# Step sizes as logarithms in the decay arguments, pair inputs as plain copies on ScalarE, output products ahead of the turn

## The chip, the cores and the metric

The kernel runs on one core of a Trainium2 chip. The metric is the device time of one launch in microseconds (us). The engines are named as in the profile: PE (matrix products and transposes; PEld is its weight load), DVE (vector), ACT (scalar functions and copies), POOL (GpSimd) and SP (issues the DMAs). They run side by side and wait for each other on semaphores.

## The reference, cut to what matters

Two batches of 1024 tokens with 256 features go through four blocks: local and global attention, a ternary feed-forward block, a state-space mixer with 64 heads, and a sum of eight factors. The change touches the mixer alone:

```python
dt = jax.nn.softplus(dt_raw + dt_bias)              # step size per token and head
a = jnp.exp(-jnp.exp(A_log) * dt)
phi = jnp.cumsum(dt, axis=1)[..., None] * rope_freqs
Bh = _rope(Bh, phi); Ch = _rope(Ch, phi)
u = xh * dt[..., None]
# per token:  h = a * h + u (outer) b ;  y = h . c
y = SSD_SCALE * ys + D_param[None, None, :, None] * xh
```

## The kernel before

Everything is written by hand: each engine has one program, and semaphores order them. A loop over the two batches holds the four blocks one after the other. In the mixer the 64 heads are worked in 32 pairs (`PAIRS`), one pair per **slot**; tokens are cut into chunks of 64 (`Q`). Ahead of the slots stands a **preparation**: `CUM` is the running sum of the step sizes, `LH` its product with the head's rate (the logarithm of the decay), `WH` the logarithm of the decay to a chunk's end. `LH` is split into three bf16 parts `LP`, stored to DRAM and loaded again in other layouts: `MV` (rows for the phases and the decays) and `NL` (the same decays as weights, for the source side of `exp(LH[t] - LH[s])`).

What each engine does in slot n, in program order:

- **DVE**: `products(n)` (L1152 to L1155, rotated B and C), `mixing(n-1)` (decay matrix times gram matrix, L1184, and the scan over chunk sums, L1189), `reduce_turns(n+2)` (L1139); in every second slot, from here on the odd one, also `pair_outputs` (L1198 to L1203) and `inputs` (L1169, L1173, L1177).
- **ACT**: `spread_decays` (L809), `whole_turns(n+2)` (L798), `turn_copy` 0 (L817), `sines(n+2)` (L804), `out_copy(n-1)` (L833), `decays(n)` (L825, an exponential), `turn_copy` 1 (L817). Sine and exponential each bring an ACT_TABLE_LOAD.
- **PE**: `turn` 0 (four transposes, L1531), `outputs(n-1)` (L1579, L1585), `decay_args(n)` (L1518, L1520), `gram` 0 (L1546), `turn` 1, `gram` 1, `phases(n+3)` (L1505), `chunk_sums(n)` (L1562), `turn_outputs(n-1)` (L1602).
- **POOL**: adds up the products: L635 for B (PE's `turn` waits for it), L636 for C (the `gram` and DVE's next `products` wait for it).
- **SP**: `swap(n+2)` (L527), four DMAs that exchange rows of the sines.

`inputs` writes what a pair of slots feeds to PE: `UI` is x times `DT8` (step size times 1/8), `US` is x times `DTW` (`DT8` times the decay to the chunk's end), and it multiplies x by `D_param` in place. The scratch `parts_d` is the DRAM copy of `LP`. `outputs(n-1)` waits for the scan of pair n-1 (`s_ss`); `products(n)` waits for `outputs(n-2)` (`s_yt`) and for POOL's L636 of slot n-1 (`s_bc`); `decay_args(n)` for `reduce_turns(n+2)` (`s_zw`); `phases(n+3)` for `decays(n)` (`s_de`), since they share two PSUM banks; `chunk_sums(n)` for `turn_copy` 1.

Of the kernel before, what the change touches and what calls it, by code (L numbers as in the profile page):

```python
# [21 lines left out]
F32 = mybir.dt.float32  # L22
# [8 lines left out]
ARENA = 39168  # L31
# [90 lines left out]
def build(nc, x, wq, wk, wv, wo, w_fc, w_proj, w_in, w_out, dt_bias, a_log, d_param, b_bias, c_bias, freqs, norm_w,  # L122
# [8 lines left out]
    with ctx:  # L131
# [131 lines left out]
        DT8 = arena.take(NT, HEADS)  # L263
        DTW = arena.take(NT, HEADS)
# [14 lines left out]
        LRES = arena.take(T)  # L279
# [4 lines left out]
        RST = arena.take(T)  # L284
# [28 lines left out]
        parts_d = nc.dram_tensor("parts_scratch", (P, 4, T), BF16, kind="Internal").ap()  # L313
        turns_d = nc.dram_tensor("turns_scratch", (PAIRS, 3, 8, P), BF16, kind="Internal").ap()
# [75 lines left out]
        s_lp = sem("parts_ready")  # L390
        s_lc = sem("chunk_decays_masked")
# [57 lines left out]
        def _(sp):  # L449
# [37 lines left out]
            with sp.Fori(0, NB) as b:  # L487
# [25 lines left out]
                for lo, hi, done in ((0, 1, s_mv0), (1, PAIRS // 4, s_mv)):  # L513
                    for q in range(3):
                        sp.dma_start(MV[32 * q:32 * q + 32, lo:hi], cum[:, lo:hi]).then_inc(done, 16)
                    sp.dma_start(MV[96:128, lo:hi], low[:, lo:hi]).then_inc(done, 16)
                    if lo == 0:
                        for a in range(3):
                            sp.dma_start(NL[64 + 16 * a:80 + 16 * a], parts_d[HEADS:, a].rearrange("h (k s) -> k h s", s=Q)
                                         ).then_inc(s_nl, 16)  # L520
# [27 lines left out]
        def _(pool):  # L548
# [45 lines left out]
            with pool.Fori(0, NB) as b:  # L594
# [29 lines left out]
                for half in range(2):  # L624
# [4 lines left out]
                    pool.drain().then_inc(s_hs, 1)  # L629
                def slots(it):  # L630
# [13 lines left out]
        def _(act):  # L644
# [29 lines left out]
            with act.Fori(0, NB) as b:  # L674
# [105 lines left out]
                nc.scalar.activation(DTE, DTE, ACT.Ln, bias=1.0).then_inc(s_lg, 1)  # L780
                act.wait_ge(s_lh, b + 1)
# [52 lines left out]

                def slots(it, first, last):
                    for k in range(4):
# [10 lines left out]
                        turn_copy(n, k, 1)  # L847

                for k in range(2):
                    whole_turns(k, k)  # L850
                    sines(k, k)
                slots(0, True, False)
# [26 lines left out]
        def _(dve):  # L879
# [103 lines left out]
            with dve.Fori(0, NB) as b:  # L983
# [85 lines left out]
                for u in range(2 * HK):  # L1069
# [22 lines left out]
                nc.vector.scalar_tensor_tensor(DT[:, :, 0], DTA, 0.0, DTE, ALU.max, ALU.add)  # L1092
                nc.vector.scalar_tensor_tensor(DT[:, :, 1], DTA, 0.0, DTE, ALU.max, ALU.add).then_inc(s_dt, 1)
# [6 lines left out]
                nc.vector.tensor_tensor_scan(CUM, RST, PS[:, 4:6, :].rearrange("p k t -> p (k t)"), 0.0, ALU.mult, ALU.add)  # L1100
# [3 lines left out]
                lh = LH[64:128].rearrange("h (k s) -> h k s", s=Q)  # L1104
                nc.vector.tensor_tensor(WH[64:128].rearrange("h (k s) -> h k s", s=Q),
                                        lh[:, :, Q - 1:Q].to_broadcast([HEADS, T // Q, Q]), lh, ALU.subtract).then_inc(s_lh, 1)
# [25 lines left out]
                nc.vector.tensor_tensor(DTW, DT8, WT, ALU.mult).then_inc(s_prep, 1)  # L1132
# [24 lines left out]
                def inputs(n, k):  # L1157

                    dve.wait_ge(s_zc, at(b, n, 3))
                    dve.wait_ge(s_yt, at(b, n, 3))  # L1160
                    m = k // 2 % 2
                    x = XS[:, :, bass.ds(n * 16, 32)]
                    each = x.rearrange("p t (r h d) -> p t r h d", r=2, h=2)
                    all4 = x.rearrange("p t (e d) -> p t e d", d=HD)
                    for c in range(2):
                        for h in range(2):
                            q, t = slice(64 * c, 64 * c + 64), slice(64 * h, 64 * h + 64)
                            f = DT8[q, :, bass.ds(n * 2, 4)].rearrange("p t (r h) -> p t r h", h=2)[:, :, :, h]
                            nc.vector.tensor_tensor(UI[t, 2 * m:2 * m + 2, c, h].rearrange("p r d t -> p t r d"),  # L1169
                                                    each[q, :, :, h], f.unsqueeze(3).to_broadcast([64, NT, 2, HD]), ALU.mult)  # L1170
                    for c in range(2):
                        q = slice(64 * c, 64 * c + 64)
                        nc.vector.tensor_tensor(US[q, m, :, :, :, :, c].rearrange("p t r h d -> p t (r h) d"), all4[q],  # L1173
                                                DTW[q, :, bass.ds(n * 2, 4)].unsqueeze(3).to_broadcast([64, NT, 4, HD]), ALU.mult)
                    dve.drain()
                    d = dpar[:, bass.ds(n * 2, 4)].unsqueeze(1).unsqueeze(3).to_broadcast([P, NT, 4, HD])
                    nc.vector.tensor_tensor(all4, all4, d, ALU.mult).then_inc(s_u, 2)  # L1177

# [14 lines left out]
                def pair_outputs(n):  # L1193
# [3 lines left out]
                    y = PS[:, 7, :].rearrange("p (y t e d) -> p y t e d", y=2, t=NT, d=HD)  # L1197
                    nc.vector.tensor_tensor(YT, y[:, 0], e, ALU.mult)  # L1198
# [3 lines left out]
                    own = XS[:, :, bass.ds(n * 16, 32)].rearrange("p t (e d) -> p t e d", d=HD)  # L1202
                    nc.vector.tensor_tensor(own, own, YT, ALU.add).then_inc(s_yd, 2)  # L1203

                def slots(it, first, last):
                    for k in range(4):
# [8 lines left out]
                        if k % 2 == 1 and not (last and k == 3):  # L1215
                            inputs(n + 1, k + 1)
# [512 lines left out]
```

## Time and profile before

| | |
|---|---|
| median of 3 runs | 1911.16 us (1909.46 to 1920.73) |
| the profiled execution | 1920.04 us, span 1918.2 us |
| mean granted PE clock | 0.803 of full |
| busy in the span | PE 1342.2, PEld 799.2, DVE 1227.5, ACT 909.1, POOL 407.5 us |
| first and last slot of the first batch begin at | 522.2 and 888.8 us |
| first and last slot of the second batch begin at | 1449.8 and 1815.5 us |

The span is the time from the first instruction to the last. An engine's busy time is a sum over stages with different limits, so it does not tell what limits the slots; for that the timeline of one pair of slots is read. A row's bracket gives the idle time of the engine before it and what ended it.

### The profile page before, as it was taken

The numbers are of one execution on the slowest core, as the hardware profiler recorded it, in microseconds if no ns is written. First come the engines' busy times: TensorE is split into PE (matmuls) and PEld (weight loads), VectorE is DVE, ScalarE is ACT, GpSimd is POOL, SyncE is SP. The second block draws the span as 40 slices with busy tenths as digits, with TensorE's granted clock in tenths as the row PEclk, the third lists the DMA queues.
The fourth block names the chain that finished last, engine by engine and source line by source line (L and its number), as shares of the span: only waits on it lengthen the run. The fifth ranks groups of instructions, "written<-read, shape, count | busy, mean of one in ns | idle before, by whom it ended". The sixth has DMA issues, their size and how long they took to land.

```text
span 1918.2 us, 40292 instructions
## 1 busy us (share of the span) xinstructions
PE 1342.2 (70%) x14984; PEld 799.2 (42%) x14984; DVE 1227.5 (64%) x2325; ACT 909.1 (47%) x1424; POOL 407.5 (21%) x322
## 2 busy tenths in 40 slices
PE   0368898595377777777637788859565777777782
PEld 0253332243155555555425333214233555555562
DVE  7456781413788888886455577342457888888836
ACT  0273456232466666664317245533145666666540
POOL 6210000020043333343012000002002333333400
PEclk9677999797577777778867689979776887777795
DMA  4300000100411111111010000010013121111100
GB/s 158 95 1 2 2 2 1 44 1 11 91 45 46 44 44 44 44 44 24 1 45 1 2 2 2 2 44 1 11 36 87 45 47 44 44 44 44 34 1 22
DMA packets 36685, 62.42 MB, mean 33 GB/s; under 512 B 15040, under 2 KB 24000, under 8 KB 35792
## 3 DMA queue, kind: packets, MB, share of 16 engines
q1 hardware_dynamic: 36272, 58.70, 12.4%
q8 instruction: 74, 1.21, 0.3%
q10 hardware_dynamic: 288, 2.10, 0.3%
q14 instruction: 51, 0.42, 0.1%
HBM read 20.79 MB, written 6.23 MB: 14 GB/s over the span
## 4 chain that ended last, share of the span: by engine, by line
issue 75%; POOL 15%; DVE 3%; POOLq 3%; PE 3%; DVEq 1%; DMA 0%; ACT 0%; SPq 0%
POOL region L636 8%; POOL region L635 6%; POOLq L628 2%; POOL region L620 1%; PE PS L1649 1%; PE PS L1664 1%; PE PS L1670 1%; DMA region<-in_L_ffn_W_proj_dram 0%; DVE fsum L976 0%; POOLq L601 0%; DVE bst L885 0%; DVE X L937 0%; DVE region L963 0%; DVE region L971 0%; DVE region L966 0%
## 5 line engine op out<-in xcount | busy, mean ns | idle before, releaser
L635 POOL TENSOR_TENSOR region<-region 128x1024 f32<-128x1024 f32 x64 | 150.8, 2356 | 655.2 <-DVE region L1155 655.2
L1018 DVE TENSOR_REDUCE region<-PS 128x1 f32<-128x512 f32 (+3 forms) x304 | 180.6, 654 | 81.5 <-PE PS L1352 44.3
L1531 PE MATMUL PS<-ident,region 128*128 128x128 f32 x512 | 102.4, 333 | 175.8 <-POOL region L635 175.8
L716 ACT ACTIVATE region<-PS 128x512 f32<-128x512 f32 x288 | 164.0, 597 | 129.1 <-PE PS L1399 88.0
L1546 PEld LDWEIGHTS PS<-region 64*64 64x64 f32 x4096 | 144.6, 141 | 47.5 <-issue 47.5
L1546 PE MATMUL PS<-region 64*64 64x64 f32 x4096 | 162.2, 230 | 0.0
L627 POOL TENSOR_TENSOR region<-region 128x512 f32<-128x512 f32 x28 | 35.4, 1265 | 553.2 <-ACT region L758 552.3
L1152 DVE SCALAR_TENSOR_TENSOR region<-region,rows 128x1024 f32<-128x1024 f32 x64 | 82.2, 1285 | 109.9 <-PE PS L1585 90.5
L1288 PE MATMUL PS<-ident,S 128*128 128x128 f32 x128 | 35.0, 429 | 167.8 <-DVE S L915 164.8
L636 POOL TENSOR_TENSOR region<-region 128x1024 f32<-128x1024 f32 x64 | 151.7, 2370 | 0.0
L817 ACT COPY region<-PS 128x512 f32<-128x512 f32 x128 | 74.9, 585 | 159.3 <-PE PS L1531 158.8
L1531 PEld LDWEIGHTS PS<-ident,region 128*128 128x128 f32 x512 | 65.0, 163 | 190.5 <-POOL region L635 94.6
L798 ACT ACTIVATE region<-PS,roundc 128x1024 f32<-128x1024 f32 x64 | 71.3, 1114 | 135.9 <-DVE region L1155 121.7
L1349 PE MATMUL PS<-region 96*128 96x512 bf16 (+3 forms) x384 | 116.4, 354 | 23.8 <-DVE region L1018 15.8
L1399 PE MATMUL PS<-region 99*128 99x512 bf16 x288 | 113.0, 415 | 18.9 <-ACT region L716 17.8
L649 ACT COPY XT<-PS 128x256 f32<-128x256 f32 x64 | 23.8, 372 | 168.0 <-PE PS L1288 166.2
L1288 PEld LDWEIGHTS PS<-ident,S 128*128 128x128 f32 x128 | 19.3, 203 | 183.3 <-DVE S L915 175.8
L1337 PE MATMUL PS<-region 128*32 128x512 f32 x576 | 86.7, 666 | 0.2
L1139 DVE SCALAR_TENSOR_TENSOR region<-region,PS 128x1024 f32<-128x1024 f32 x64 | 76.8, 1200 | 12.7 <-ACT region L798 12.7
L1184 DVE TENSOR_TENSOR S<-PS,region 128x1024 f32<-128x1024 f32 x64 | 78.1, 1221 | 9.7 <-PE PS L1546 9.0
L1155 DVE SCALAR_TENSOR_TENSOR region<-region,rows 128x1024 f32<-128x1024 f32 x64 | 81.9, 1280 | 0.0
L1154 DVE SCALAR_TENSOR_TENSOR region<-region,rows 128x1024 f32<-128x1024 f32 x64 | 81.9, 1280 | 0.0
(246 smaller groups left out, 2960.1 us busy)
## 6 DMA issues: line engine op xcount, KB each, us to landing
region<-region SPq DMA_DIRECT2D x256, 128.0 KB, 2.3
region<-parts_scratch SPq DMA_DIRECT2D x8, 448.0 KB, 9.2
region<-in_L_ffn_factors_dram SPq DMA_DIRECT2D x2, 1024.0 KB, 7.3
X<-in_L_attn_x_dram SPq DMA_DIRECT2D x2, 1024.0 KB, 5.9
region<-w1T_scratch SPq DMA_DIRECT2D x2, 1024.0 KB, 4.8
region<-w2T_scratch SPq DMA_DIRECT2D x2, 1024.0 KB, 6.9
out_dram<-X SPq DMA_DIRECT2D x2, 1024.0 KB, 4.9
parts_scratch<-region SPq DMA_DIRECT2D x2, 768.0 KB, 3.2
```

Source lines behind the costliest of these rows:

```text
L635: nc.gpsimd.tensor_tensor(PB1[:, r], PB1[:, r], PB2, ALU.add).then_inc(s_bb, 1)
L636: nc.gpsimd.tensor_tensor(PC1[:, r], PC1[:, r], PC2, ALU.add).then_inc(s_bc, 1)
L716: nc.scalar.activation(PB[:, u % (2 * G0), :], PS[:, 2 + u % 2, :], ACT.Exp).then_inc(s_p, 1)
L1018: nc.vector.reduce_max(MB[:, h:h + nh, k0 // 4], src, AX).then_inc(s_smu, 1)
L1152: nc.vector.scalar_tensor_tensor(PB1[:, k % 2], XV[:, 0], g(0), T1[:, k % 2], ALU.add, ALU.mult)
L1154: nc.vector.scalar_tensor_tensor(PC1[:, k % 2], XV[:, 2], g(2), T1[:, k % 2], ALU.add, ALU.mult)
L1155: nc.vector.scalar_tensor_tensor(PC2, XV[:, 3], g(3), T2[:, k % 2], ALU.add, ALU.mult).then_inc(s_pm, 1)
L1337: mm(PS[32 * g:32 * g + 32, 4, :], V[:, j, g, :], PB[:, v % (2 * G0), :], start=j == 0, stop=j == i, tile_position=(0, 32 * g), skip_group ...
L1349: last = mm(o, QT[0:SPLIT, h + q, i * P:(i + 1) * P], KT[0:SPLIT, (h + q) // HPG, k0 * P:(k0 + nk) * P], start=True, stop=not diag, skip_g ...
L1399: last = mm(o, KT[:, g, j * P:(j + 1) * P], QT[:, g * HPG:(g + 1) * HPG, i * P:(i + 1) * P], start=True, stop=j != i)
L1531: last = tr(PS[:, 4, (i % 4) * P:(i % 4 + 1) * P], PB1[:, r, i * P:(i + 1) * P], ident[:])
L1546: last = mm(PS[q, 2 + half, (i % 4) * P + 64 * c:(i % 4) * P + 64 * c + 64], PB1[q, r, t], PC1[q, r, t], start=True, stop=True, tile_posit ...
```

## The change

Three things are changed. First, the step size leaves the inputs: `exp(LH[t] - LH[s]) * dt[s] / 8` becomes `exp(LH[t] - (LH[s] - log(dt[s] / 8)))`. The preparation gains a logarithm on ACT (`LN`), a subtraction on DVE (`LS`), a split of `LS` into three bf16 parts on POOL (`LQ`), and a DRAM round trip of its own for the source side (`sources_d`, then `NL`), and SP issues that after all loads of `MV`. `XW`, x times the decay to the chunk's end, is made once for all heads on DVE. Second, `inputs` then only copies, and moves from DVE to the end of the odd slots on ACT; the product with `D_param` goes into DVE's `pair_outputs`. Third, PE does `outputs(n-1)` ahead of `turn` 0 in a slot.

```diff
 (SP, preparation: the NL loads no longer stand between the first and the other loads of MV)
+                sp.wait_ge(s_lq, b + 1)
+                sp.dma_start(sources_d, LQ[64:128]).then_inc(s_lqs, 16)
+                sp.wait_ge(s_lqs, (b + 1) * 16)
+                for a in range(3):
+                    sp.dma_start(NL[64 + 16 * a:80 + 16 * a], sources_d[:, a].rearrange("h (k s) -> k h s", s=Q)
+                                 ).then_inc(s_nl, 16)
 (POOL, preparation)
+                pool.wait_ge(s_lh, b + 1)
+                nc.gpsimd.tensor_tensor(LQ[64:128, 0], LS[64:128], onesc[64:128].to_broadcast([HEADS, T]), ALU.mult)
+                pool.drain()
+                nc.gpsimd.tensor_tensor(LS[64:128], LS[64:128], LQ[64:128, 0], ALU.subtract)
+                pool.drain()
+                nc.gpsimd.tensor_copy(LQ[64:128, 1], LS[64:128])
+                pool.drain()
+                nc.gpsimd.tensor_tensor(LQ[64:128, 2], LS[64:128], LQ[64:128, 1], ALU.subtract).then_inc(s_lq, 1)
 (ACT, preparation)
+                act.wait_ge(s_cum, b + 1)
+                nc.scalar.activation(LN[64:128], PS[64:128, 4:6, :].rearrange("p k t -> p (k t)"), ACT.Ln,
+                                     scale=float(NS) ** -0.5).then_inc(s_ln, 1)
 (ACT, at the end of a slot with k = 1 or 3)
+                    for c in range(2):
+                        for h in range(2):
+                            nc.scalar.copy(UI[t, 2 * m:2 * m + 2, c, h].rearrange("p r d t -> p t r d"), x[q, :, :, h])
+                    for c in range(2):
+                        last = nc.scalar.copy(US[q, m, :, :, :, :, c].rearrange("p t r h d -> p t (r h) d"), w[q])
 (DVE, preparation)
-                nc.vector.tensor_scalar(DT8, DT[:, :, 0], float(NS) ** -0.5, None, ALU.mult)
+                dve.wait_ge(s_ln, b + 1)
+                nc.vector.tensor_tensor(LS[64:128], LH[64:128], LN[64:128], ALU.subtract)
...
-                nc.vector.tensor_tensor(DTW, DT8, WT, ALU.mult).then_inc(s_prep, 1)
+                nc.vector.tensor_tensor(XW.rearrange("p t (h d) -> p (t h) d", d=HD), XS.rearrange("p t (h d) -> p (t h) d", d=HD),
+                                        WT.rearrange("p t h -> p (t h)").unsqueeze(2).to_broadcast([P, NT * HEADS, HD]),
+                                        ALU.mult).then_inc(s_prep, 1)
 (DVE, slots: inputs is gone; in pair_outputs)
                     nc.vector.tensor_tensor(YT, y[:, 0], e, ALU.mult)
+                    nc.vector.tensor_tensor(own, own, d, ALU.mult)
                     dve.drain()
 (PE, slots)
-                        turn(n, k, 0)
                         if not (first and k == 0):
                             outputs(n - 1, k + 3)
+                        turn(n, k, 0)
                         decay_args(it, k, not (last_ and k >= 2))
```

In the order of PE's instructions this is the beginning of a slot inside the loop; before (`PS<-ident,region` is `turn`, 32x128 are `outputs`, 128x512 are `decay_args`, 64x64 is `gram`):

```order
L1531 MATMUL PS<-ident,region 128x128 x4
L1579 MATMUL PS<-region 32x128 x8
L1585 MATMUL PS<-S,region 32x128 x8
...
L1518 MATMUL PS<-region 128x512
L1520 MATMUL PS<-region 128x512
L1518 MATMUL PS<-region 128x512
L1520 MATMUL PS<-region 128x512
L1546 MATMUL PS<-region 64x64 x16
```

and after:

```order
L1602 MATMUL PS<-region 32x128 x8
L1608 MATMUL PS<-S,region 32x128 x8
L1551 ISA
L1554 MATMUL PS<-ident,region 128x128 x4
...
L1541 MATMUL PS<-region 128x512
L1543 MATMUL PS<-region 128x512
L1541 MATMUL PS<-region 128x512
L1543 MATMUL PS<-region 128x512
L1569 MATMUL PS<-region 64x64 x16
```

The sixteen `outputs` products moved ahead of the four transposes; the rest of the slot stands as it stood.

On ACT the end of an odd slot and the beginning of the next, after the change (`x4` and `x2` are the new copies to `UI` and `US`, L838 is `turn_copy`, L830 `spread_decays`, L819 `whole_turns`):

```order
L846 ACTIVATE region<-PS 128x1024
L835 REGISTER_ALU
L838 COPY region<-PS 128x512
L865 COPY region<-region 64x8x2x8 x4
L869 COPY region<-region 64x256 x2
L830 COPY region<-region 128x16x15
L816 REGISTER_ALU
L819 ACTIVATE region<-PS,roundc 128x1024
```

Before, `spread_decays` followed `turn_copy` 1 at once. On SP, in the preparation, before:

```order
L507 DMA parts_scratch<-region 128x3072
L509 REGISTER_ALU
L515 DMA region<-parts_scratch 32x1024 x3
L516 DMA region<-parts_scratch 32x1024
L519 DMA region<-parts_scratch 16x64x64 x3
L515 DMA region<-parts_scratch 32x7x1024 x3
L516 DMA region<-parts_scratch 32x7x1024
L525 ISA
L527 DMA region<-region 32x1024 x4
```

and after:

```order
L513 DMA parts_scratch<-region 128x3072
L515 REGISTER_ALU
L521 DMA region<-parts_scratch 32x1024 x3
L522 DMA region<-parts_scratch 32x1024
L521 DMA region<-parts_scratch 32x7x1024 x3
L522 DMA region<-parts_scratch 32x7x1024
L525 DMA sources_scratch<-region 64x3072
L528 DMA region<-sources_scratch 16x64x64 x3
L534 ISA
L536 DMA region<-region 32x1024 x4
```

The three loads of `NL` (16x64x64) moved behind the big loads of `MV` and behind a store of their own, and stand directly ahead of the first `swap`.

## Rows read from the trace of the kernel before

**Rows 1.** What DVE waited for before the first product of a slot (us, times).

```profile
L1152 DVE SCALAR_TENSOR_TENSOR region<-region,rows x64: 1279/1285/1287, 522.2 to 1815.5; 128x1024 f32<-128x1024 f32 x64
...
  PE PS L1585: 90.5, 30
```

**Rows 2.** Timeline, DVE: first and last slot of batch one, first of two.

```profile
522.18 1.28 DVE L1152 SCALAR_TENSOR_TENSOR region<-region,rows 128x1024 f32<-128x1024 f32 x1 [3.73 <-DMA region<-region]
...
888.82 1.28 DVE L1152 SCALAR_TENSOR_TENSOR region<-region,rows 128x1024 f32<-128x1024 f32 x1 [3.95 <-PE PS L1585]
...
1449.78 1.28 DVE L1152 SCALAR_TENSOR_TENSOR region<-region,rows 128x1024 f32<-128x1024 f32 x1 [3.06 <-DMA region<-region]
```

**Rows 3.** Timeline of an even slot (start, duration in us, engine, line).

```profile
715.17 1.28 DVE L1155 SCALAR_TENSOR_TENSOR region<-region,rows 128x1024 f32<-128x1024 f32 x1
...
718.84 2.37 POOL L636 TENSOR_TENSOR region<-region 128x1024 f32<-128x1024 f32 x1
...
719.02 1.11 PE L1531 MATMUL PS<-ident,region 128*128 128x128 f32 x4 [4.75 <-POOL region L635]
...
720.06 1.11 PE L1579 MATMUL PS<-region 128*32 128x128 f32 x16
...
721.96 0.61 PE L1518 MATMUL PS<-region 112*128 112x512 bf16 x1
...
722.30 1.28 DVE L1152 SCALAR_TENSOR_TENSOR region<-region,rows 128x1024 f32<-128x1024 f32 x1 [3.00 <-PE PS L1585]
...
727.58 1.10 PE L1562 MATMUL PS<-region 128*64 128x16 f32 x32
```

**Rows 4.** Timeline of the odd slot that follows.

```profile
728.73 0.69 DVE L1189 TENSOR_TENSOR_SCAN region<-region,PS 128x256 f32<-128x256 f32 x1 [0.36 <-PE PS L1562]
...
729.67 0.66 PE L1531 MATMUL PS<-ident,region 128*128 128x128 f32 x4 [0.42 <-POOL region L635]
730.25 0.45 PEld L1579 LDWEIGHTS PS<-region 128*32 128x32 f32 x16 [0.17 <-issue]
...
731.37 0.39 PE L1518 MATMUL PS<-region 112*128 112x512 bf16 x1
...
731.52 0.72 DVE L1203 TENSOR_TENSOR region<-region 128x256 f32 x1 [0.17 <-issue]
...
732.17 1.59 DVE L1169 TENSOR_TENSOR region<-region 64x128 f32 x4
...
734.06 1.20 PE L1546 MATMUL PS<-region 64*64 64x64 f32 x32
...
735.24 1.28 DVE L1152 SCALAR_TENSOR_TENSOR region<-region,rows 128x1024 f32<-128x1024 f32 x1
...
736.42 0.60 PE L1505 MATMUL PS<-region 96*128 x2 [1.17 <-ACT region L825]
736.49 0.41 ACT L809 COPY region<-region 128x240 f32 x1
...
736.95 1.11 PE L1562 MATMUL PS<-region 128*64 128x16 f32 x32
```

**Rows 5.** Two windows: length, busy per engine, then granted clock, DMA, GB/s.

```profile
714.50:724.70 10.20, 5.68 (x57) 3.54 (x59) 7.20 (x8) 5.60 (x6) 4.67 (x2) 0.50 0.05 11
724.80:738.30 13.50, 11.91 (x260) 9.32 (x258) 12.64 (x18) 9.60 (x13) 4.71 (x2) 1.00 0.30 68
```

**Rows 6.** Timeline, batch two: POOL's addition and DVE's input products beside it.

```profile
1466.85 2.38 POOL L636 TENSOR_TENSOR region<-region 128x1024 f32<-128x1024 f32 x1
...
1467.21 3.47 DVE L1169 TENSOR_TENSOR region<-region 64x128 f32<-64x128 f32 x4
```

**Rows 7.** Timeline, preparation of batch one: DVE, the subtraction to WH.

```profile
492.14 1.22 DVE L1105 TENSOR_TENSOR region<-region 64x1024 f32<-64x1024 f32 x1
```

**Rows 8.** DMA issues by line (count, KB each, us to landing).

```profile
parts_scratch<-region SPq DMA_DIRECT2D x2, 768.0 KB, 3.2
...
region<-parts_scratch SPq DMA_DIRECT2D x6, 128.0 KB, 4.8
```

More of the change, by code:

```diff
@@ L30 @@
 BLOCKS = 4
-ARENA = 39168
+ARENA = 41984
 C = 256
@@ L262, in build @@
         XV = arena.take(4, T)
-        DT8 = arena.take(NT, HEADS)
-        DTW = arena.take(NT, HEADS)
+        XW = arena.take(NT, DI)
         ELT = arena.take(NT, HEADS)
@@ L278, in build @@
         LH = arena.take(T)
-        LRES = arena.take(T)
+        LRES = BSQ.rearrange("p t n -> p (t n)")
         LP = arena.take(3, T, dt=BF16)
@@ L283, in build @@
         LCH = arena.take(PAIRS, T // Q)
-        RST = arena.take(T)
+        LQ = arena.take(3, T, dt=BF16)
+        RST = LQ.rearrange("p q t -> p (q t)").bitcast(F32)[:, 0:T]
+        LN, LS = WH, CUM
         prep_used = arena.used
@@ L390, in build @@
         s_lp = sem("parts_ready")
+        s_cum = sem("sums_of_steps_ready")
+        s_ln = sem("log_steps_ready")
+        s_lq = sem("source_parts_ready")
+        s_lqs = sem("source_parts_stored")
         s_lc = sem("chunk_decays_masked")
@@ L833, in out_copy, with inputs @@
                     nc.scalar.copy(YC[:, k % 2], PS[:, 6, :]).then_inc(s_yc, 1)
+                def inputs(n, k):
+                    act.wait_ge(s_zc, at(b, n, 3))
+                    act.wait_ge(s_yt, at(b, n, 3))
+                    m = k // 2 % 2
+                    x = XS[:, :, bass.ds(n * 16, 32)].rearrange("p t (r h d) -> p t r h d", r=2, h=2)
+                    for c in range(2):
+                        for h in range(2):
+                            q, t = slice(64 * c, 64 * c + 64), slice(64 * h, 64 * h + 64)
+                            nc.scalar.copy(UI[t, 2 * m:2 * m + 2, c, h].rearrange("p r d t -> p t r d"), x[q, :, :, h])
+                    w = XW[:, :, bass.ds(n * 16, 32)].rearrange("p t (e d) -> p t e d", d=HD)
+                    for c in range(2):
+                        q = slice(64 * c, 64 * c + 64)
+                        last = nc.scalar.copy(US[q, m, :, :, :, :, c].rearrange("p t r h d -> p t (r h) d"), w[q])
+                    last.then_inc(s_u, 2)
                 def slots(it, first, last):
@@ L847, in slots @@
                         turn_copy(n, k, 1)
+                        if k % 2 == 1 and not (last and k == 3):
+                            inputs(n + 1, k + 1)
                 for k in range(2):
@@ L851, in _ @@
                     sines(k, k)
+                act.wait_ge(s_prep, b + 1)
+                inputs(0, 0)
                 slots(0, True, False)
@@ L1155, in products @@
                     nc.vector.scalar_tensor_tensor(PC2, XV[:, 3], g(3), T2[:, k % 2], ALU.add, ALU.mult).then_inc(s_pm, 1)
[L1157 to L1177, printed above, removed]
                 def mixing(n, k):
@@ L1214, in slots @@
                             pair_outputs(n - 3)
-                        if k % 2 == 1 and not (last and k == 3):
-                            inputs(n + 1, k + 1)
                 reduce_turns(0, 0)
                 reduce_turns(1, 1)
-                inputs(0, 0)
                 slots(0, True, False)
```

21 lines of the change are left out of this document (10 added, 11 removed).

## The prediction

> **What bounds the kernel now.** I look first at DVE's first product of a slot. It began 366.64 us after the first in the last slot of batch one (31 slots, 11.83 us each), and in batch two from 1449.78 to 1815.5, 11.80 each [rows 1, 2]. So 62 slot steps of 11.81 us hold 732 of the 1920 us; two slots are 23.6 us. Next I ask what DVE waited for there: 90.5 us in 30 slots for PE's outputs [rows 1]. The timeline shows the chain of a pair. DVE's products end at 716.45 (715.17 + 1.28); POOL adds for 2 x 2.4 us, to 721.21; PE turns B from 719.02, does the outputs from 720.06 to 721.96, and DVE goes on at 722.30 after 3.00 us idle [rows 3]. Then DVE works almost without a gap until the next products at 735.24, the last 3.07 us of it inputs (from 732.17) [rows 4]. Neither PE nor ACT is full: ACT is busy 5.60 + 9.60 = 15.2 us of the pair [rows 5]. The pair is one chain: products, POOL, turn, outputs, products, inputs.
>
> **Part one: inputs leave DVE.** DVE loses 3.07 us in an odd slot and gains the product with D_param in pair_outputs, 256 elements, some 0.4 us. That product reads two operands in SBUF. Such an operation stands still beside POOL: four input products took 3.47 us beside L636 against 1.59 alone, and L1203 took 0.72 [rows 4, 6]. Pair_outputs starts some 3.3 us after the products' end, L636 ends 4.76 after it (721.21 - 716.45), so the product and the two operations behind it end near 4.76 + 0.3 + 0.5 + 0.5 = 6.0; with products of 4.87 an odd slot needs 10.9 us on DVE. An even slot needs L636 and then products: 4.76 + 0.1 + 4.87 = 9.7. DVE and POOL alone would allow 20.6 per pair, 10.3 per slot.
>
> **Part two: six copies on ACT.** The nearest row is a copy of 240 elements, 0.41 us [rows 4]; six of those are 2.46. DVE's own figure, 1.59 + 0.85, is the same. Four of the copies have only 128 elements, so I take 2.2, with 2.0 to 2.5 as bounds; in slots 15.2 + 2.2 = 17.4 us per pair, under the 20.6. They stand beside work of others: from turn_copy 1 to the next turn_copy 0, ACT has 2.2 + 0.41 + 1.1 = 3.7 us, while PE and DVE have chunk sums, scan, outputs and turn, 0.3 + 1.11 + 0.8 + 1.1 + 0.7 = 4.0. Cover for 0.3; beyond 2.5 us every tenth would show. The Trainium skill (ScalarE: Activation LUTs, section "What ACT_TABLE_LOAD costs") gives an ACTIVATE 186 ns plus 0.833 ns per element, less 93 when back to back; by that estimate the six take 1.4 us, and the cover would be 1.1. No number here uses it.
>
> **Part three: outputs first.** DVE's 3.00 us shrink only to the next lock, L636 at 4.76, so 2.0. But a new ring closes: scan, outputs, turn, ACT's copies, sine and exponential, phases, chunk sums, scan. Before, the turn waited for POOL alone. At the high clock: outputs 731.37 - 730.25 = 1.12; turn to the end of the chunk sums 729.67 to 738.06 = 8.39, all of it ACT's sequence and what PE hangs on it; scan 0.69 plus 0.2 of semaphores [rows 4]. Sum **10.4 us** per slot, just over DVE's 10.3. At the low clock outputs take 721.96 - 720.06 = 1.90, and turn to end of chunk sums 719.02 to 728.68 = 9.66 [rows 3]: 1.90 + 9.66 + 0.89 = **12.45**. In between, with only outputs and turn low: 1.12 becomes 1.90 and the turn 1.11 instead of 0.66, so 10.4 + 0.78 + 0.45 = **11.63**.
>
> **The clock decides.** It is the high level (2.4 GHz) from 724.8 to 738.3 and the low one (1.2) from 714.5 to 724.7 [rows 5]. It fell at 738.3 after PE had idled 1.17 us for the exponential and then done only phases, chunk sums and turn_outputs, and rose 5.7 us after work began at 719.02. In the new ring at the high clock PE's gram ends 735.26 - 729.67 = 5.59 after the old turn; without the outputs between, 4.5. The phases start 6.75 after the turn (736.42 - 729.67): a hole of 2.2 us, then the same light work. So I expect a fall in most slots that began at the high clock; the next slot then has outputs and turn at the low one, its gram ends about when the exponential does, the hole closes and the clock comes back. Half high at 10.4 and half at 11.63 gives 11.0; I take **11.05**. Loop: 62 x (11.81 - 11.05) = **-47 us**.
>
> **Part four: the preparation.** It ends, before, with DVE waiting 3.73 us for the first swap, behind the loads of MV in the queue [rows 2]. Per batch:
> DVE gains the subtraction LS, 1.2 us [rows 7]; the logarithm (1.0, like an exponential of the size) runs beside LH; DT8 goes, -0.3. Together +1.2 ahead of LP.
> POOL gains three additions and a copy over 1024 elements, 4 x 2.4 = 9.5 us, beside five DVE operations on LP, two or three of them with both operands in SBUF. By rows 6 each of those waits out a POOL operation: two to three waits of 2.4, 4.7 to 7.1; 0 if POOL comes late. I take 6. The Trainium skill (SBUF — State Buffer, section "Who interferes with whom") makes the pair of ports an exclusive lock for a whole instruction and adds that casts in a two-port mode take it too; by that the two casts to LP wait as well, and the estimate is the upper bound, 7.1. No row here shows a cast beside POOL.
> SP now waits for the store of LQ behind all MV loads: a round trip like that of LP, 3.2 us [rows 8], half the bytes. The NL loads (4.8 us [rows 8]) and the swap follow as before, only later.
> XW is a product of 4096 elements, four times 1.2 less overheads, 4.4 us instead of 0.7: hidden behind the queue, which is then some ten us late; without that cover it would cost 3.7.
> Sum 1.2 + 6 + 3.2 = 10.4 per batch (4.4 to 12): **+21 us**.
>
> **Forecast.** Against the profiled 1920.04 us (its span is 1918.2) the sum is -26; it stands 9 us over the median, inside the runs' spread, and I carry the -26 over: 1911 - 26 = **1885 us**, own range 1870 to 1900. Less than 1%, 19 us, cannot be told from no change here.
>
> **Rivals.**
> (a) The clock stays high: the fall above came with DVE idle for another 4.75 us behind it, and the new ring has no such pause. For it: 10.4 per slot; 62 x 1.41 = 87, less 21: 1911 - 66 = 1845. Against: the clock fell at 738.3 before that pause had its turn. 27%.
> (b) Every slot at 11.63, the hole not closing: 62 x 0.18 = 11 off, 21 on: 1921, no change. 13%.
> (c) Slower: outputs now run in front of turn, decay_args and gram, all at the low clock, and PE itself becomes the ring. If slots alternate between 11.63 and 12.45, mean 12.04: +14 and +21, 1946. It decides from a mean slot of 11.5, where the loop no longer pays for the preparation; +1% is reached at 11.8. For: at the low clock the gram ended after the exponential in rows 3's slot. Against: without a hole PE is busy, and in rows 5 that brought the clock back. 11%.
> (d) The strided copies cost twice the rows, 4.4 us: 1.9 over the cover, in 31 pair steps of both batches 59 us on top of the forecast: 1944. Against: DVE's 1.59 already holds the strided writes. 6%.
> The forecast keeps 43%.
>
> **How the numbers follow.** Faster by over 1% (under 1892) holds (a) and three quarters of the forecast's share: 0.58. Same (to 1930): the rest of it and (b): 0.25. Slower: (c), (d): 0.17. The range leaves out the tail beyond (a) and that beyond (c): 1840 to 1945.
>
> **What the changed profile would show.** Steps of 11.0 us between first products, alternating by about 1.2; PE's first outputs row waiting for DVE's scan, not for POOL; the granted clock in the loop near 0.8 and low at outputs; six ACT copies of 2.0 to 2.5 us together, and no wait of DVE for whole_turns; DVE's LRES and LP operations stretched beside POOL, and the first products some 10 us later after LP's store. The forecast is wrong if the slots are at 10.4 or over 11.5, or if the preparation moves by less than 3 us or more than 13.

## The result, and the profile after

The changed kernel takes **1922.49 us** (median of 12 runs, 1917.98 to 1930.04), the kernel before 1911.88 beside it (12 runs, 1906.02 to 1920.73). The ratio is 1.0054, 95% interval [1.0035, 1.0073]. It is a little slower and not, as forecast, faster. The profiled execution has a span of 1925.8 us at a mean granted clock of 0.807 (before 1918.2 and 0.803).

The timeline of DVE in the changed kernel, four single answers: the first product of the first and the last slot of batch one, then of batch two. They answer to [rows 2].

```profile
532.32 1.28 DVE L1198 SCALAR_TENSOR_TENSOR region<-region,rows 128x1024 f32<-128x1024 f32 x1 [8.98 <-DMA region<-region]
...
894.29 1.28 DVE L1198 SCALAR_TENSOR_TENSOR region<-region,rows 128x1024 f32<-128x1024 f32 x1 [2.36 <-PE PS L1608]
...
1462.40 1.28 DVE L1198 SCALAR_TENSOR_TENSOR region<-region,rows 128x1024 f32<-128x1024 f32 x1 [7.90 <-DMA region<-region]
...
1822.66 1.28 DVE L1198 SCALAR_TENSOR_TENSOR region<-region,rows 128x1024 f32<-128x1024 f32 x1 [2.36 <-PE PS L1608]
```

31 slots in 361.97 and 360.26 us are steps of 11.68 and 11.62 us. Before they were 11.83 and 11.80: the loop gained 4.7 and 5.4 us per batch, 10 in all, where 47 were forecast. Most of that lies in its start: the first four steps of a batch took 45.9 us before and 41.4 and 41.5 now, while from the eighth slot on the mean step went from 11.94 and 11.91 to 11.89 and 11.88. The loop once it runs has gained next to nothing. The preparation, from the start of the cumulative scan at 489.33 (L1140) to the first product, took 532.32 - 489.33 = 43.0 us, and 41.9 in batch two; before it was 33.2 and 32.5. That is 19 us more. The two together, 9 us more, are the result.

The loop first. What DVE waited for before L1198, whole span (us, times); it answers to [rows 1], where 90.5 us in 30 slots stood:

```profile
L1198 DVE SCALAR_TENSOR_TENSOR region<-region,rows x64: 1277/1284/1286, 532.3 to 1822.7; 128x1024 f32<-128x1024 f32 x64
...
  PE PS L1608: 12.8, 15
  POOL region L654: 9.3, 5
```

The wait that outputs first was made for is down to a seventh. The same view for `phases` on PE (it adds the idle time of PE's weight load) shows another:

```profile
L1528 PE MATMUL PS<-region x128: 379/387/634, 516.0 to 1806.3; 96*128 x96, 96*128 96x512 bf16 x32
...
  ACT region L846: 122.3, 64
```

Before, this row read 20.1 us in 21. PE alone, counted in the timeline, now waits for ACT's exponential (L846) ahead of 56 of the 58 `phases` inside the slots, 108 us, 1.9 us each; before it was 17 us ahead of 17 of them. The timeline of an odd slot with its predecessor's end shows what hangs on it. It answers to [rows 3, 4]: L1554 is `turn`, L1602 and L1608 `outputs`, L1585 `chunk_sums`, L1213 DVE's scan.

```profile
721.86 1.00 PE L1528 MATMUL PS<-region 96*128 x2 [2.25 <-ACT region L846]
...
722.06 1.75 ACT L865 COPY region<-region 64x128 f32 x4
...
722.78 1.88 PE L1585 MATMUL PS<-region 128*64 128x16 f32 x32
723.82 0.86 ACT L869 COPY region<-region 64x256 f32 x2
...
724.71 0.69 DVE L1213 TENSOR_TENSOR_SCAN region<-region,PS 128x256 f32<-128x256 f32 x1 [1.55 <-PE PS L1585]
...
725.60 1.11 PE L1602 MATMUL PS<-region 128*32 128x128 f32 x16
...
727.49 1.11 PE L1554 MATMUL PS<-ident,region 128*128 128x128 f32 x4
...
731.26 1.20 PE L1569 MATMUL PS<-region 64*64 64x64 f32 x32
...
733.38 1.02 ACT L846 ACTIVATE region<-PS 128x1024 f32<-128x1024 f32 x1
...
734.57 0.60 PE L1528 MATMUL PS<-region 96*128 x2 [2.11 <-ACT region L846]
...
735.10 1.51 PE L1585 MATMUL PS<-region 128*64 128x16 f32 x32
...
736.65 0.69 DVE L1213 TENSOR_TENSOR_SCAN region<-region,PS 128x256 f32<-128x256 f32 x1 [0.93 <-PE PS L1585]
...
737.53 1.11 PE L1602 MATMUL PS<-region 128*32 128x128 f32 x16
...
739.25 0.65 PE L1554 MATMUL PS<-ident,region 128*128 128x128 f32 x4
```

From turn to turn it is 739.25 - 727.49 = 11.76 us. PE ends its gram at 732.46 and stands idle until 734.57. In the kernel before, in the slot of [rows 3], the second gram ended at 727.11, 8.09 us after the turn, and `phases` (L1505) came without a hole:

```profile
725.91 1.20 PE L1546 MATMUL PS<-region 64*64 64x64 f32 x32
...
727.04 0.60 PE L1505 MATMUL PS<-region 96*128 x2
```

Windows of the changed kernel's stretch (length, busy of PE, PEld, DVE, ACT, POOL, granted clock, DMA share, GB/s; they answer to [rows 5]):

```profile
721.90:728.60 6.70, 6.70 (x87) 5.23 (x88) 3.89 (x4) 4.13 (x9) 4.33 (x2) 0.50 0.09 20
729.00:735.40 6.40, 4.27 (x82) 3.05 (x83) 4.62 (x5) 6.20 (x9) 2.61 (x2) 1.00 0.36 82
736.00:738.90 2.90, 2.90 (x56) 2.74 (x58) 2.25 (x4) 0.43 (x1) 1.45 (x1) 0.50 0.00 0
```

In this slot the clock is at 2.4 GHz for decay arguments, grams, hole and `phases`, and at 1.2 GHz for most of the chunk sums and for the outputs. In the slot before it `phases`, chunk sums and outputs all ran at 1.2. That is the work that the ring runs through.

The preparation, timeline of batch one in the changed kernel. L1159 and L1161 are DVE's last operations on the way to `LP`, L640 begins the split on POOL, L1176 is `XW`, L525 the source's store, L528 the loads of `NL`, L536 the swaps.

```profile
495.31 2.40 POOL L640 TENSOR_TENSOR region<-region,onesc 64x1024 bf16<-64x1024 f32 x1 [74.30 <-DVE region L1149]
...
501.66 1.31 DVE L1159 CAST region<-region 128x1024 bf16<-128x1024 f32 x1
...
503.05 2.99 DVE L1161 TENSOR_TENSOR region<-region 128x1024 bf16<-128x1024 f32 x1
...
513.01 0.81 SPq L525 DMA_DIRECT2D sources_scratch<-region  x1
...
514.29 4.42 DVE L1176 TENSOR_TENSOR region<-region 128x4096 f32<-128x4096 f32 x1
...
523.89 1.63 SPq L528 DMA_DIRECT2D region<-sources_scratch  x3
...
525.65 19.33 SPq L536 DMA_DIRECT2D region<-region  x12
```

`LP` is complete at 506.04, 16.7 us after the scan's start (before 10.2). The source's store is issued behind the loads of `MV`, its `NL` loads 10.9 us later, and the first swap behind those.

### The profile page after: what moved, and what is told of

Same layout as the page of the kernel before. It is cut to its first block, busy times and chain, and to the rows that moved or that the text cites. A ratio compares the mean times of both kernels' runs of the same rounds, so it can differ in the third digit from the quotient of the medians.

```text
span 1925.8 us, 40168 instructions
## 1 busy us (share of the span) xinstructions
PE 1360.6 (71%) x14904; PEld 840.1 (44%) x14984; DVE 1162.5 (60%) x2133; ACT 987.4 (51%) x1618; POOL 425.9 (22%) x330
## 3 DMA queue, kind: packets, MB, share of 16 engines
q1 hardware_dynamic: 36432, 59.48, 12.5%
## 4 chain that ended last, share of the span: by engine, by line
issue 65%; PE 11%; POOL 8%; ACT 6%; DVE 4%; POOLq 4%; DVEq 1%; DMA 0%; ACTq 0%; SPq 0%
POOL region L654 4%; POOL region L653 3%; PE PS L1585 2%; POOLq L637 2%; ACT L825 2%; PE PS L1602 2%; PE PS L1554 2%; ACT L846 2%; ACT region L846 2%; PE PS L1608 1%; PE PS L1625 1%; POOL region L629 1%; PE PS L1528 1%; PE PS L1672 1%; ACT region L854 1%
## 5 line engine op out<-in xcount | busy, mean ns | idle before, releaser
L838 ACT COPY region<-PS 128x512 f32<-128x512 f32 x128 | 74.6, 583 | 189.8 <-PE PS L1554 189.8
L1569 PEld LDWEIGHTS PS<-region 64*64 64x64 f32 x4096 | 137.3, 135 | 44.5 <-issue 44.5
L1569 PE MATMUL PS<-region 64*64 64x64 f32 x4096 | 154.8, 224 | 1.2 <-issue 1.1
L1528 PE MATMUL PS<-region 96*128 (+1 forms) x128 | 45.4, 442 | 121.6 <-ACT region L846 108.2
L1554 PE MATMUL PS<-ident,region 128*128 128x128 f32 x512 | 104.1, 337 | 29.8 <-POOL region L653 29.8
L1198 DVE SCALAR_TENSOR_TENSOR region<-region,rows 128x1024 f32<-128x1024 f32 x64 | 82.1, 1283 | 46.3 <-DMA region<-region 16.9
L1585 PEld LDWEIGHTS PS<-region 128*64 128x64 f32 x2048 | 88.5, 178 | 34.0 <-ACT region L838 31.5
L1585 PE MATMUL PS<-region 128*64 128x16 f32 (+1 forms) x2048 | 94.4, 237 | 5.2 <-ACT region L838 5.2
L1554 PEld LDWEIGHTS PS<-ident,region 128*128 128x128 f32 x512 | 66.8, 167 | 57.1 <-issue 52.7
```

Source lines behind the costliest of these rows:

```text
L1198: nc.vector.scalar_tensor_tensor(PB1[:, k % 2], XV[:, 0], g(0), T1[:, k % 2], ALU.add, ALU.mult)
L1554: last = tr(PS[:, 4, (i % 4) * P:(i % 4 + 1) * P], PB1[:, r, i * P:(i + 1) * P], ident[:])
L1569: last = mm(PS[q, 2 + half, (i % 4) * P + 64 * c:(i % 4) * P + 64 * c + 64], PB1[q, r, t], PC1[q, r, t], start=True, stop=True, tile_posit ...
L1585: last = mm(to[:, 8 * h:8 * h + 8, 2 * i:2 * i + w], BT[:, r, i, 64 * h:64 * h + 64], US[:, m, i, r, h, :, 0:w], start=True, stop=True, ti ...
```

## Experiments

Ten kernels ran, each timed in three rounds beside the kernel before. "Slot" is the mean step between first products of batch one and two, "preparation" the time from the scan's start to the first product, both read as above; the clock is the mean of the profiled execution. A ratio is to the kernel before in the same rounds (1913.6 to 1914.6 us for e1 to e10).

| kernel | median us | ratio [95%] | slot | preparation | clock |
|---|---|---|---|---|---|
| before | 1911.9 | 1 | 11.83, 11.80 | 33.2, 32.5 | 0.803 |
| changed | 1922.5 | 1.0054 [1.0035, 1.0073] | 11.68, 11.62 | 43.0, 41.9 | 0.807 |
| e1 | 1867.8 | 0.9775 [0.9741, 0.9810] | 10.79, 10.83 | 42.9, 41.8 | 0.832 |
| e2 | 1914.7 | 1.0013 [0.9989, 1.0037] | 11.86, 11.88 | 31.7, 33.1 | 0.817 |
| e3 | 1867.2 | 0.9768 [0.9737, 0.9799] | 10.62, 10.62 | 41.1, 41.4 | 0.882 |
| e4 | 1912.5 | 0.9993 [0.9967, 1.0018] | 11.67, 11.66 | 37.1, 37.1 | 0.807 |
| e5 | 1862.8 | 0.9725 [0.9683, 0.9766] | 10.77, 10.73 | 37.1, 37.1 | 0.824 |
| e6 | 1860.6 | 0.9712 [0.9668, 0.9756] | 10.77, 10.80 | 37.1, 37.4 | 0.829 |
| e7 | 1859.0 | 0.9720 [0.9680, 0.9760] | 10.63, 10.72 | 37.1, 37.1 | 0.831 |
| e8 | 1853.8 | 0.9681 [0.9641, 0.9722] | 10.67, 10.71 | 37.1, 37.1 | 0.846 |
| e9 | 1860.8 | 0.9732 [0.9681, 0.9783] | 10.72, 10.68 | 39.1, 39.5 | 0.852 |
| e10 | 1860.7 | 0.9724 [0.9672, 0.9775] | 10.64, 10.64 | 39.5, 39.6 | 0.875 |

Slot and preparation come from one profiled execution each. What lies outside of them took 1106 to 1125 us in these twelve executions, so a difference of a few us between medians of four or five runs need not come from the edit. The profiled execution lies under its kernel's median by 12 us in e3 and by 8 in e9, and over it by 9 in e8 and by 5 in e5.

**e1: the changed kernel with PE's old order.**

```diff
+                        turn(n, k, 0)
                         if not (first and k == 0):
                             outputs(n - 1, k + 3)
-                        turn(n, k, 0)
```

> The changed kernel with PE's turn ahead of the outputs in a slot, as before the change; all else as changed. Theory R (the ring through outputs): a slot of the changed kernel is as long as the ring scan, outputs, turn, ACT's sequence, phases, chunk sums, scan, 11.65 us on average. With turn first the outputs leave the ring and also fill part of PE's hole ahead of the phases. Expected: 10.6 to 11.2 us per slot, so 28 to 65 us less than the changed kernel's 1922: 1857 to 1894 us. Rival L (DVE beside POOL's lock, or ACT with its six copies, sets the slot): the order on PE does not matter, 1915 to 1925 us.

One moved call takes 55 us off the changed kernel. The theory of the ring held: preparation as before the edit, slot 0.8 us shorter. PE's wait before `phases` fell from 122.3 to 32.2 us in the view above. In the odd slots DVE and POOL show as the limit that part one of the prediction described; timeline of one:

```profile
716.85 2.38 POOL L654 TENSOR_TENSOR region<-region 128x1024 f32<-128x1024 f32 x1
...
717.55 1.97 DVE L1225 TENSOR_TENSOR region<-region,dpar  x1
...
720.54 1.28 DVE L1198 SCALAR_TENSOR_TENSOR region<-region,rows 128x1024 f32<-128x1024 f32 x1
```

The product with `D_param` takes 1.97 us beside POOL and 0.41 without it (738.70 in the changed kernel). The step to the next products is 10.96 us, with DVE at work all the time; part one gave 10.9. In the even slots DVE still waited for PE's outputs, 25 us in 10 of the last 24 slots of batch one.

**e2: the kernel before with outputs first, and nothing else.**

```diff
-                        turn(n, k, 0)
                         if not (first and k == 0):
                             outputs(n - 1, k + 3)
+                        turn(n, k, 0)
```

> The kernel before with nothing changed but PE's order: outputs ahead of turn. Theory R: the ring of 11.6 us per slot (clock low at phases, chunk sums, outputs) now bounds the even slots that took 10.7, and the odd slots stay at DVE's 12.9: a pair of 24.0 to 24.5 us against 23.6, 10 to 28 us slower, 1922 to 1940 us. Rival G (the reorder is what its place suggests, a shorter way from POOL to DVE's products): DVE's 3.0 us of idle time shrink to 2.0, 1880 to 1895 us.

No gain, and the time, 1914.7, lies below the theory's range and far above the rival's. DVE's wait fell only to POOL's addition, and the hole ahead of `phases` (here L1505) opened. Timeline, the end of an odd slot and the even one behind it:

```profile
704.93 1.28 DVE L1152 SCALAR_TENSOR_TENSOR region<-region,rows 128x1024 f32<-128x1024 f32 x1 [0.60 <-PE PS L1546]
...
706.62 1.03 PE L1505 MATMUL PS<-region 96*128 x2 [2.25 <-ACT region L825]
...
714.71 1.28 DVE L1152 SCALAR_TENSOR_TENSOR region<-region,rows 128x1024 f32<-128x1024 f32 x1 [2.06 <-POOL region L636]
```

From the even slot's first product to the next slot's it is 9.78 us; the odd slot behind it takes 13.9, and the pair is at 23.7 as before. The theory had the ring lengthen the even slot; the odd one lengthened and the even one shortened. With e1 this makes a square. Everything but the order, mainly inputs on ACT, is worth 1.0 us per slot with turn first (before to e1) and 0.2 with outputs first (e2 to changed); the order by itself brings nothing, and with the copies it takes most of their gain away.

**e3: PE's hole filled.** Sixteen products go to columns of `PS` that nothing reads in the slots; they compute nothing that is used.

```diff
                         gram(n, k, 1)
+                        for _ in range(16):
+                            mm(PS[:, 5, 272:512], identb[:], masks[:, 0:240], start=True, stop=True)
```

> The changed kernel with sixteen extra bf16 products of 240 columns on PE behind the second gram of every slot, written to columns of PSUM that nothing reads: they fill the hole in which PE waits for the exponential. Theory C (the clock): the ring is 10.4 us at the high clock, and what makes it 11.65 is that the clock falls in or behind the hole, so that phases, chunk sums and outputs run at the low one. Expected: granted clock in the slots over 0.95, phases 0.6, chunk sums 1.1, outputs 1.1 us, slots of 10.3 to 10.7 us, 1840 to 1870 us. Rival N (the ring's length is set by ACT and the semaphores, not by the clock): the extra products only delay the phases, 1922 to 1960 us.

Work that is useless takes 55 us off, as theory C gave and against rival N. Windows and timeline of e3:

```profile
532.00:890.00 358.00, 315.87 (x5617) 246.97 (x5618) 273.58 (x287) 276.52 (x385) 149.12 (x64) 0.99 0.20 45
```

```profile
719.37 1.81 PE L1640 MATMUL PS<-masks,identb 128*128 128x240 bf16 x16
721.81 0.60 PE L1528 MATMUL PS<-region 96*128 x2 [0.63 <-ACT region L846]
722.35 1.10 PE L1585 MATMUL PS<-region 128*64 128x16 f32 x32
...
724.24 0.70 PE L1602 MATMUL PS<-region 128*32 128x128 f32 x16 [0.23 <-DVE region L1213]
...
725.36 0.66 PE L1554 MATMUL PS<-ident,region 128*128 128x128 f32 x4
```

In the loop of batch one the granted clock is 0.99, where the changed kernel had 0.79. From `phases` to the turn it is 725.36 - 721.81 = 3.55 us; the changed kernel had 727.49 - 721.86 = 5.63 and 739.25 - 734.57 = 4.68. That is where the slot's time went. What is left here of DVE's idle time is, in the last 24 slots of batch one, 21.5 us in 11 slots for `whole_turns`, which stands behind the six copies on ACT, and 20.6 in 19 for the chunk sums.

**e4: the split on POOL waits for `LP`.**

```diff
-                pool.wait_ge(s_lh, b + 1)
+                pool.wait_ge(s_lp, b + 1)
```

> The changed kernel with POOL's split of LS waiting until DVE has finished LP, so that its four operations no longer run beside DVE's operations on SBUF operands. Theory P (POOL holds DVE up in the preparation): LP is stored 5 to 6 us earlier in each batch, the split is ready at about the time at which SP has issued the loads of MV, and the kernel takes 9 to 12 us less than the changed one: 1910 to 1914 us. Rival Q (the DMA queue alone sets when the first products start): under 3 us, 1919 to 1923 us.

Theory P held. `LP` was complete 11.65 us after the scan's start, not 16.7: 5.06 us were contention. The preparation took 5.9 and 4.9 us less, and the median 10.0. The loop stayed as it was. The contention did not vanish, it moved, to small operations with one array and one column as operands (L1161 ends `LP`, L1171 is such an operation):

```profile
503.71 1.23 DVE L1161 TENSOR_TENSOR region<-region 128x1024 bf16<-128x1024 f32 x1
...
505.05 1.91 DVE L1171 TENSOR_SCALAR region<-region,rstd 128x64 f32<-128x64 f32 x1
```

The 48 of them took from 504.85 to 519.51, 14.7 us, against 8.3 in the changed kernel (505.96 to 514.29).

**e5: e1 and e4 together.** Diffs as there.

> The changed kernel with PE's turn first and with POOL's split waiting for LP: the two edits of the first runs together. Both are in different stages, so they should add: the slots of 10.8 us of the run with the turn first (1868) and a preparation of 37.1 us instead of 42. Expected 1856 to 1862 us. Rival: the preparation's gain is lost when the first slots wait for something else, 1866 to 1870.

Slot of e1, preparation of e4: in the profile the two add up. The median, 1862.8, is just above the expected range.

**e6: e5, and the large loads of `MV` issued behind the first two swaps.**

```diff
+                load_rows(0, 1, s_mv0)
...
                 swap(0, 0)
                 swap(1, 1)
+                load_rows(1, PAIRS // 4, s_mv)
```

> The run before (turn first, split late) with the big loads of MV issued behind the first two swaps instead of ahead of the sources' round trip. Theory Q: what remains of the longer preparation is the queue, in which the first swap stands behind the MV loads, a store's round trip and NL. Expected: first products some 30 us after the start of the running sum instead of 37, 14 us less in all, 1842 to 1848 us. Rival: the preparation is then set by DVE's product XW, the sines and the NL loads, and gains less than 3 us per batch, 1853 or more.

A miss: the queue was cleared and the preparation stayed at 37.1. The timeline of e6 (lines three further on: L1179 is `XW`, L1188 `reduce_turns`, L828 the sine, L538 the swap, L530 the `NL` loads):

```profile
507.93 1.53 SPq L530 DMA_DIRECT2D region<-sources_scratch  x3
...
511.24 4.41 DVE L1179 TENSOR_TENSOR region<-region 128x4096 f32<-128x4096 f32 x1
...
515.57 1.20 DVE L1188 SCALAR_TENSOR_TENSOR region<-region,PS 128x1024 f32<-128x1024 f32 x1
...
516.81 1.06 ACT L828 ACTIVATE region<-region 128x1024 f32<-128x1024 f32 x1 [0.69 <-DVE region L1188]
...
517.89 5.90 SPq L538 DMA_DIRECT2D region<-region  x8
...
522.10 1.28 DVE L1201 SCALAR_TENSOR_TENSOR region<-region,rows 128x1024 f32<-128x1024 f32 x1 [1.83 <-DMA region<-region]
```

Nothing stood in the queue when the sine ended; the swap went out at once. The limit was engines' work, DVE's chain of small operations, `XW` and `reduce_turns`, then the sine. It had been so since e4: there too `XW` began 26.2 us after the scan's start (at 519.51), and the swap went out at 526.17, when the sine was done. The edit cleared a queue that no longer set the time.

**e7: e6, with the ACT copies behind `whole_turns`** in the even slots instead of at the end of the odd ones (`inputs(n, k)` ahead of `turn_copy(n, k, 0)`).

> The run before with ACT's six copies moved from the end of the odd slot to the next slot behind whole_turns, ahead of the turn's copy. Theory A: at 2.6 us the copies outlast their cover and hold back whole_turns, so DVE's reduce_turns and PE's decay arguments start late in every even slot (DVE waited 0.7 us for ACT there, 2.1 with the high clock). With whole_turns first that wait goes: slots of 10.5 instead of 10.8 us, 12 to 22 us less than the run before, 1822 to 1834. Rival: the copies then stand before the turn's copy, which opens ACT's sequence, and delay it by as much: no change within 5 us, or slower.

A miss; the rival held. The slots are shorter by 0.14 and 0.07 us, the median by 1.5; the intervals overlap, and no gain is shown. DVE's wait for `whole_turns` did go (7.7 us in the last 24 slots of e6's batch one, none here), but its wait for POOL's addition ahead of the products grew from 2.3 to 16.2.

**e8: e7 with eight filling products** at e3's place.

> The run before with eight extra bf16 products of 240 columns behind the second gram (half of those of the first such run, since the outputs already stand in the slot's first half). Theory C: the clock still falls in part of the slots with the turn first (0.83 over the kernel), and with the hole half filled it stays high: granted clock in the slots over 0.95 and 10.2 to 10.4 us per slot, 6 to 18 us less than the run before. Rival: with the turn first PE's hole is no longer in the ring and the clock does not matter, no change or some us slower.

A miss: the loop's clock rose from 0.87 (e7) to 0.92 and not over 0.95, and the slot did not get shorter. The rival fits. The median is the lowest of all, 3.2% under the kernel before; that it beats e5 to e7 is not shown, since the intervals overlap and loop and preparation together of both batches are as in e7 (736.8 against 736.0 us). Windows of e8 and, in the second line, of e10 below:

```profile
532.00:880.00 348.00, 296.44 (x5306) 221.56 (x5306) 282.13 (x284) 270.76 (x369) 150.10 (x64) 0.92 0.23 51
...
532.00:880.00 348.00, 302.10 (x5533) 239.63 (x5566) 271.20 (x283) 270.38 (x369) 150.47 (x64) 0.99 0.21 48
```

**e9: e8 with `XW` behind the first two `reduce_turns`.** The array `WT` that it reads lies elsewhere in memory, and a drain follows it.

```diff
-                nc.vector.tensor_tensor(XW ... )
...
                 reduce_turns(0, 0)
                 reduce_turns(1, 1)
+                nc.vector.tensor_tensor(XW ... )
```

> The kernel of e8 with DVE's product XW (4.4 us) moved behind the first two reduce_turns, ahead of the first products; the array that it reads is placed elsewhere, so that the first swap may land before XW has ended. Theory D, the preparation is set by DVE's own chain: in e6 XW ended at 515.65, reduce_turns followed at 515.57, the sine at 516.81, the swap was issued at 517.89 and had landed by 522.10. Without XW in that chain the swap is issued 4.4 us sooner, XW lies beside sine and swap, and the preparation takes 37.1 - 4.4 = 32.7 us per batch (31.5 to 34), 8 to 9 us less in all: 1845 (1841 to 1850). Rival, the queue: SP issued the loads of NL at 507.93 in e6 and they need some 5 us; with the swap behind them in the queue the preparation moves by under 2 us per batch, 1850 to 1855. A second rival: DVE reaches XW late, since reduce_turns 1 waits for ACT's second round (2.27 us idle in e6), and the first products then wait for XW: half of the 4.4 comes back, 34.5 to 35.5.

A miss: the preparation became 2.0 and 2.5 us longer. Timeline of e9 (L1184 is `reduce_turns`, L1244 `XW`):

```profile
512.21 1.11 ACT L822 ACTIVATE region<-PS,roundc 128x1024 f32<-128x1024 f32 x1 [0.93 <-PE PS L1532]
...
513.36 1.22 DVE L1184 SCALAR_TENSOR_TENSOR region<-region,PS 128x1024 f32<-128x1024 f32 x1 [3.41 <-ACT region L822]
...
517.99 4.42 DVE L1244 TENSOR_TENSOR region<-region 128x4096 f32<-128x4096 f32 x1
```

Against the scan's start the first `reduce_turns` began at 513.36 - 483.65 = 29.7 us, in e6 at 515.57 - 485.00 = 30.6. Only 0.9 of `XW`'s 4.4 had been on the path: the rest lay beside PE's transposes and ACT's copies, up to `whole_turns` (L822). Behind `reduce_turns` it ends at 522.41 and the first product follows at 522.76. My theory D fell; the second rival is what happened, and cost more than it had said.

**e10: all of e9's preparation, but PE's order of the changed kernel,** the copies at their place, and sixteen filling products. So it differs from e9 in the order, the copies' place and the number of filling products.

> The changed kernel with its order in PE's slot kept (outputs first), 16 filling products behind the second gram as in e3, the split of LS on POOL behind LP, the large loads of MV behind the first swaps, and XW behind the first two reduce_turns. Theory C: once PE's hole is filled, the granted clock is near 1 in the loop and the order of turn and outputs costs nothing: slots of 10.6 to 10.7 as in e3, preparation as in e9, so 1867 - 2 x (41.3 - 32.7) = 1850 (1843 to 1856), within 0.5% of e9. Rival: outputs first costs something by itself (PE's turn hangs on DVE's scan), and slots are 10.9 or more beside those of e9: 1862 or more, or the other way round, the clock at 0.99 in place of 0.92 shortens the slot below e9's by over 0.15 us: 1840 or less.

The time is e9's, at a loop clock of 0.99 against 0.91. It lies 5 us above the expected range, since the preparation missed as in e9; the slots, 10.64, are what the theory gave. With the hole filled outputs first costs nothing, nor does it bring anything, as far as a comparison can tell in which three things differ.

## Why the prediction was wrong

The forecast was 1885, 26 us faster; the kernel became 11 us slower. The 1922 lie outside the forecast's own range of 1870 to 1900, inside the wide one of 1840 to 1945, and at the number of rival (b), 1921, which had 13%. Its own sign of being wrong, slots over 11.5 us, is there. That the number of (b) is met so closely is in part luck: its condition, the hole not closing, held, but the mean of 11.65 is made of a short start and of 11.9 from the eighth slot on.

**What bounds the kernel now:** right as a description of the chain. Taking the inputs out of it (before to e1) made a slot 1.0 us shorter. Taking out DVE's wait for the outputs alone (e2) brought nothing, since the new ring took its place.

**Part one, DVE and POOL:** right for the odd slots. The product with `D_param` is held by POOL in e1 as described, and every second odd slot of e1, e3 and e8 took 10.95 us in the loop's middle, where 10.9 was given; the other, in which the loop of four slots turns round, took 11.53. The even slots were given 9.7 and took 9.9 to 10.8. So the fastest loops stand at 10.6, not 10.3.

**Part two, the copies:** 1.75 + 0.86 = 2.6 us against 2.2, above the upper bound of 2.5. The estimate from the Trainium skill (ScalarE: Activation LUTs, section "What ACT_TABLE_LOAD costs"), 1.4 us, was further off; each of the six took 0.43. In the changed kernel they were hidden even so, since PE's chain does not pass them: DVE waited 0.89 us for `whole_turns` behind them, beside PE's outputs, and still 0.33 for the outputs. With the hole filled (e3) they showed: DVE waited 1.8 to 2.1 us there in an even slot.

**Part three and the clock:** the ring closed as described. Between the levels 11.63 was given, 11.76 was measured in the slot above. The step that failed is "the next slot then has outputs and turn at the low one, its gram ends about when the exponential does, the hole closes and the clock comes back". That the gram ends with the exponential was read from [rows 3], where the outputs stood between turn and gram and took 1.90 us of PE at the low clock. The change takes them out of just that place. The exponential hangs on the turn, and so the gram now ends 732.46 - 727.49 = 4.97 us after the turn, not 8.09, and `phases` start at 7.08. I had subtracted the outputs for the high clock ("without the outputs between, 4.5") and not for the low one. Of the 3.1 us, 1.9 are the outputs. The other 1.2 come from the clock, which rose 1.3 us after this turn began (in [rows 3] 5.7), so that decay arguments and first gram ran at 2.4 GHz: the clock did come back, but ahead of the hole, and made it longer. A hole of 1.4 to 2.4 us therefore stands in every slot of the loop's middle, at whatever clock the slot began, and the clock falls in it or behind it each time. The slots that were to take 10.4, those whose turn runs at the high clock, are not the shortest but the longest: from 595.88 to 858.52 in batch one there are six of them, 12.2 to 12.5 us from turn to turn, and the others take 11.5 to 12.2. With a mean of 11.65 the sum is 62 x 0.163 = 10 off, 19 on: the result.

A smaller error lies in the 11.63 itself: it leaves chunk sums at their duration at the high clock, 1.11 us, and they took 1.51 in the slot above and 1.88 in the one before it, since the clock falls in them or ahead of them.

**Part four, the preparation:** right in the sum, and in LS and POOL's contention. Forecast were 1.2 + 6 + 3.2 = 10.4 per batch (the upper bound of its terms is 11.5, not 12); in batch one 1.5 (11.65 - 10.16, e4's `LP` against before's), 5.06 (contention, e4) and 3.2 (26.3 us from `LP` to the first product against 23.1) make 9.8. The third is right by its size and not by what made it: the source's store, queued behind the loads of `MV`, took 10.9 us and not 3.2. The swap went out 19.6 us after `LP`'s store instead of 14.1, the time at which the sine allowed it before, and landed in 6.6 us instead of 8.9. The Trainium skill (SBUF — State Buffer, section "Who interferes with whom") counts casts among the operations that can wait, and the trace agrees: the cast at 501.66 took 1.31 us beside POOL against 0.69 in e4, where POOL was idle. `XW` was hidden, as said; e6 and e9 show that even with the queue cleared only 0.9 of it lay on the path, where 3.7 had been given for that case.

**Rivals:** (a) needed a clock that stays high, and e3 shows what that gives, with a fill that the change did not have: 1867 instead of 1845, of which 62 x (10.62 - 10.4) = 14 us are the slot. The pause of 4.75 us named there is PE's ahead of the turn [rows 3], not DVE's. (c) did not occur, since decay arguments and grams ran at the high clock in the slots shown, nor did (d): the six copies took 2.6 us, not 4.4.

What stays open: why the even slots take 9.9 to 10.4 us and not 9.7 with the clock at 0.99 (DVE's wait for `whole_turns` behind the copies is the nearest suspect; no run moves the copies with the hole filled and outputs first), and whether e8's last 5 us are more than chance.

## What to carry to other kernels

When work is moved on an engine, ask first what it had been filling at its old place: here the outputs had covered PE's wait for an exponential, and a reorder that took one wait away opened another of 2 us in each slot. A measurement of "the hole closes" holds only for the order in which it was made. Where an engine's idle time brings its clock down ahead of the work that the ring runs through, try both filling the hole and moving real work into it; in this kernel each gave 55 us, and both together (e8) no more in the slot than moving the work alone.

## What the runs showed of the hardware

- In the loop TensorE stood at a granted clock of 0.79 with holes of 2 us, and at 0.99 with sixteen bf16 products of 240 columns in them. 32 products of 16 columns took 1.88 us at 1.2 GHz and 1.10 at 2.4.
- A granted clock that rises need not buy time: in e8 and e9 it was 0.92 and 0.91, with turn ahead of outputs, against 0.87 in e7, and the slot stayed at 10.7.
- DVE is held by POOL also in an operation with one array and a column of scalars: 128x64 elements in 1.91 us (e4, beside POOL's L640) against 0.24.
- POOL pays too: its f32 subtraction over 64x1024 elements (L642) took 2.12 us in e4, where one DVE operation stood beside it for all of that time, and 2.92 in the changed kernel beside DVE's subtraction of 128x1024 elements and the product behind it, which took 2.17 and 2.77 us instead of 1.23 and 1.04.
